# A four-layer graph network on one core: sorted blocks of 2500 edges, layer norms in one ScalarE pass

## The reference, cut to what matters

```python
h = jnp.maximum(_layernorm(x), 0.0)
x = x + gcn(h)             # normalized sum over the edges, @ W.T + b
h = jnp.maximum(_layernorm(x), 0.0)
x = x + attention(h)       # 4 heads of 32, softmax over the edges of a destination
h = jnp.maximum(_layernorm(x), 0.0)
x = x + weighted(h)        # two layers with edge weights, then a projection
h = jnp.maximum(_layernorm(x), 0.0)
xw = h @ W;  ew = edge_attr_16 @ edge_w        # [3125,128], [103125,128]
x = x + segment_sum(xw[src] * ew, dst) + b     # the edge layer
```

## Time and profile before

| | us |
|---|---|
| median of 3 runs | 2925.09 |
| lowest, highest | 2921.11, 2953.8 |
| the profiled execution | 2937.53 |
| its span | 2935.8 |
| PE busy in the span | 2349.3 (80%) |
| POOL busy | 1953.1 (67%) |
| DVE busy | 1910.0 (65%) |
| ScalarE (ACT) busy | 1408.7 (48%) |

### The profile page before, as it was taken

How to read it: one execution, slowest core, us unless ns; L and a number is a source line. 1 busy time by engine, 2 the same in 40 slices (tenths; PEclk the granted TensorE clock), 3 DMA queues, 4 the chain that set the end, 5 groups by cost and what they waited for, 6 DMA issues and landing times. The chain is left out here.

```text
span 2935.8 us, 64938 instructions
## 1 busy us (share of the span) xinstructions
PE 2349.3 (80%) x22192; PEld 1710.9 (58%) x22192; DVE 1910.0 (65%) x3810; ACT 1408.7 (48%) x2659; POOL 1953.1 (67%) x1608
## 2 busy tenths in 40 slices
PE   4677777766857777777788787889978999999998
PEld 2466666663424555555555555434546777777777
DVE  7999999983457777777777787211134555556555
ACT  0498988880038777777777775000003221222211
POOL 2278878805148888778777783577605888878874
PEclk7699999988968999988888899899987998999999
DMA  6267777768421111111111112996952222222213
GB/s 83 91 173 200 190 198 189 188 186 205 110 67 49 45 44 42 43 41 45 41 41 41 42 42 37 217 217 139 212 121 63 55 53 54 55 54 55 61 46 55
DMA packets 220459, 285.63 MB, mean 97 GB/s; under 512 B 130299, under 2 KB 166530, under 8 KB 217015
## 3 DMA queue, kind: packets, MB, share of 16 engines
q1 hardware_dynamic: 171548, 246.53, 33.8%
q0 software_dynamic: 48720, 36.84, 6.4%
HBM read 171.50 MB, written 112.09 MB: 97 GB/s over the span
## 5 line engine op out<-in xcount | busy, mean ns | idle before, releaser
L389 POOL DMA_INDIRECT scratch_slots<-sort_pay,sort_slot x400 | 590.0, 1475 | 185.2 <-issue 184.3
L1864 POOL TENSOR_TENSOR score<-score,rise 125x500 f32<-125x500 f32 (+1 forms) x609 | 671.9, 1139 | 52.5 <-DVE peaks L1800 48.5
L2399 POOL DMA_INDIRECT gathered_rows<-scratch_projected,src_i x425 | 532.4, 1253 | 156.7 <-issue 126.5
L1800 DVE CUSTOM_DVE_ANT_0 score<-raw,log_in 125x500 f32<-125x500 f32 (+1 forms) x609 | 353.9, 619 | 167.6 <-PE raw L1685 97.6
L1747 ACT ACTIVATE rise<-raw 125x1000 f32<-125x1000 f32 (+1 forms) x350 | 313.4, 918 | 183.1 <-DVE peaks L1800 95.7
L1700 PE MATMUL probsT<-ident,score 125*125 125x125 f32 x2175 | 363.8, 298 | 29.6 <-ACT score L1756 13.1
L1700 PEld LDWEIGHTS probsT<-ident,score 125*125 125x125 f32 x2175 | 304.3, 204 | 110.1 <-DVE weighed L1821 65.2
L874 PE MATMUL built<-pair_weight,hot 125*128 125x125 bf16 x3750 | 249.7, 229 | 63.9 <-DVE pair_weight L819 63.7
L1685 PE MATMUL raw<-QT,key 32*125 32x500 f32 (+1 forms) x1400 | 205.1, 657 | 94.8 <-DVE peaks L1800 90.8
L874 PEld LDWEIGHTS built<-pair_weight,hot 125*128 125x128 bf16 x3750 | 229.7, 103 | 75.8 <-DVE pair_weight L819 74.2
L1821 DVE COPY weighed<-probsT 125x500 f32<-125x500 f32 x400 | 251.1, 672 | 13.6 <-PE probsT L1700 13.6
(11 more groups left out here) (309 smaller groups left out, 4484.2 us busy)
## 6 DMA issues: line engine op xcount, KB each, us to landing
weights_in<-scratch_weightsT SPq DMA_DIRECT2D x50, 1093.8 KB
scratch_weightsT<-wT SPq DMA_DIRECT2D x25, 1367.2 KB
scratch_logs<-log SPq DMA_DIRECT2D x75, 437.5 KB
log_in<-scratch_logs SPq DMA_DIRECT2D x150, 218.8 KB
counts_in<-scratch_counts SPq DMA_DIRECT2D x25, 683.6 KB
scratch_counts<-cc SPq DMA_DIRECT2D x24, 683.6 KB
gathered_rows<-scratch_projected,src_i POOLq DMA_INDIRECT x425
scratch_slots<-sort_pay,sort_slot POOLq DMA_INDIRECT x400
```

The costliest lines, as they stand in the source:

```text
L389: nc.gpsimd.indirect_dma_start(rows, bass.IndirectOffsetOnAxis(ap=sort["slot"][:, b, c:c + 1], axis=0), pay[:, c, :], None).then_inc(sort[ ...
L1800: nc.vector.tensor_tensor_reduce(out=score[u][h][:, at:at + w], in0=raw[:, h, 0:w], in1=log_in[:, at:at + w], scale=1.0, scalar=-3e38, op0 ...
L1864: nc.gpsimd.tensor_tensor(score[u][h][:, at:at + w], score[u][h][:, at:at + w], rise[:, b, h, 0:w], ALU.add).then_inc(added, 1)
L2399: nc.gpsimd.indirect_dma_start(gathered[:, g % GATHERS, k, :], None, projected, bass.IndirectOffsetOnAxis(ap=src_i[:, FIRST + g, k:k + 1], ...
```

## The change

- **Blocks.** 24 blocks of 2500 edges, 60000 edges; 28 lists, of 128 slots each, without a second half. `REACH` is 88. A block is 7 rounds of four lists, 168 rounds in all; 69 groups are left for the gathers. Two blocks are placed together (`PER_BATCH`), so there are 12 batches of again 40 scatters: six in `adjacency`, one in `regular_gcn_layer`, five in `weighted_layers`.
- **Slots.** The four lists of a round lie in SBUF with the second pair at partition 64 once turned. The mixing is two matmuls, each of 36 partitions and 256 columns, into two banks. A block's slots are loaded in two DMAs with runs of 144 bytes, into four buffers instead of two; the first two loads stand in the prelude.
- **Edge stage.** The turned attributes share a bank with the turned slots, and their turn stands ahead of the block's sum. The first three gathers stand in the prelude. The rounding of the table runs in two interleaved strands.
- **Layer norm.** DVE's 25 subtractions are gone. `lift` = -mean / deviation is a bias, and ScalarE's pass becomes `Relu(scale * X + lift)`.
- **Bias.** `L3_gnn_b` starts the sums `acc` (on POOL) instead of being added to `X` (on DVE).
- **Semaphores** of the first layer are recorded and cleared later by POOL.

```diff
-SORT_BLOCKS = 10
-COLS = 40
+BATCHES = 12
+PER_BATCH = 2
+SORT_BLOCKS = BATCHES * PER_BATCH
+COLS = 20
-LISTS = 26
+LISTS = 28
-REACH = 168
+REACH = 88
-PLACED_IN_ADJACENCY = 5
+PLACED_IN_ADJACENCY = 6
...
-        for t in range(a, b):
-            nc.vector.tensor_scalar(H[:, t, :], X[:, t, :], mv[:, t, 0:1], 0.0, ALU.subtract, ALU.max)
         dve.wait_ge(std_ready, s + 1)
-        nc.vector.reciprocal(rstd[:, a:b], rstd[:, a:b]).then_inc(inv_ready, 1)
+        link(nc.vector.reciprocal(rstd[:, a:b], rstd[:, a:b]))
+        nc.vector.scalar_tensor_tensor(lift[:, a:b], mv[:, a:b, 0], -1.0, rstd[:, a:b], ALU.mult, ALU.mult).then_inc(inv_ready, 1)
...
-                    ins = nc.scalar.activation(H[:, t, :], H[:, t, :], ACT.Copy, scale=rstd[:, t:t + 1])
+                    ins = nc.scalar.activation(H[:, t, :], X[:, t, :], ACT.Relu, bias=lift[:, t:t + 1], scale=rstd[:, t:t + 1])
...
-    for c in range(COLS):
-        nc.gpsimd.indirect_dma_start(rows, bass.IndirectOffsetOnAxis(ap=sort["slot"][:, b, c:c + 1], axis=0), pay[:, c, :],
+    for c in range(PER_BATCH * COLS):
+        nc.gpsimd.indirect_dma_start(rows, bass.IndirectOffsetOnAxis(ap=slot[:, c:c + 1], axis=0), pay[:, c, :],
                                      None).then_inc(sort["placed"][u], 16)
...
-                    ins = nc.tensor.matmul(offset_ps[:], above16[:], in_list[:, :, :, c].rearrange("p b s -> p (b s)"),
-                                           start=(c == 0), stop=(c == COLS - 1))
+                    for u in range(2):
+                        ins = nc.tensor.matmul(offset_ps[:, u, 0:BATCHES * LISTS], above16[:],
+                                               in_list[:, BATCHES * u:BATCHES * (u + 1), :, c].rearrange("p b s -> p (b s)"),
+                                               start=(c == 0), stop=(c == COLS - 1))
...
-    PER_BLOCK = LISTS // 2
+    PER_BLOCK = LISTS // QUAD
+    BLOCK_BUFFERS = 4
+    HEAD_CHUNKS = 3
...
+        def load_block(sp, b):
+            u = b % BLOCK_BUFFERS
+            by_half = slots[b].rearrange("r (j l x) w -> r j l (x w)", l=2, x=2)
+            for half in range(2):
+                at = half * SECOND_ROWS
+                sp.dma_start(pay[:, u, :, at:at + 2 * SLOT], by_half[:, :, half, :]).then_inc(slots_in[u], 16)
...
+                pool.wait_ge(last["in"], 16 * LAST_LOADS)
+                pool.wait_ge(emptied, 1)
+                nc.gpsimd.tensor_scalar(acc[:], acc[:], last["bias"][:, 0:1], None, ALU.add)
+                pool.wait_ge(stored, 32)
+                for k in range(HEAD_CHUNKS):
+                    gather_chunk(0, k)
...
-                nc.vector.tensor_tensor(X[:], X[:], bias[:].unsqueeze(1).broadcast_to([P, TILES, D]), ALU.add)
...
                 def mix_attributes(r):
                     need(pe, s_copied, r)
-                    nc.tensor.matmul(mixed_ps[:], pay_t[:, r % 2, :], quad_mix[:].rearrange("r c d -> r (c d)"), start=True,
-                                     stop=True).then_inc(s_mixed, 1)
+                    for half in range(2):
+                        rows = slice(half * SECOND_ROWS, half * SECOND_ROWS + 2 * SLOT)
+                        ins = nc.tensor.matmul(mixed_ps[:, half, 0:2 * D], pay_t[rows, r % 2, :],
+                                               quad_mix[rows].rearrange("r c d -> r (c d)"), start=True, stop=True)
+                    ins.then_inc(s_mixed, 1)
...
+                    if r == -1:
+                        turn_attributes(0)
+                    if g is not None and g + 1 < ITEMS:
+                        turn_attributes(g + 1)
                     if here(r - 1):
                         sum_block(r - 1)
-                    if r == -1:
-                        turn_attributes(0)
                     if g is not None:
                         factors(g)
-                        if g + 1 < ITEMS:
-                            turn_attributes(g + 1)
```

More of the change, by code:

```diff
@@ L352, in _ @@
             sp.dma_start(table[ROWS:ROWS + GROWS, :], pad[:]).then_inc(table_done, 16)
-            with nc.allow_non_contiguous_dma(reason="runs of forty edges, and one destination of every block"):
+            with nc.allow_non_contiguous_dma(reason="runs of twenty edges, and one destination of every block"):
                 sp.dma_start(sort["base_i"][:], T["dst"][0:SORTED].rearrange("(o b r) -> o b r", o=1, r=BLOCK_EDGES)[:, :, 0]
@@ L2272, in _ @@
                     if r >= 2:
-                        pe.wait_ge(left, 2 * (r - 2) + 1)
+                        pe.wait_ge(left, 2 * r - 3 if r > 2 else 1)
                     for s in range(s0, s0 + n):
@@ L2652, in program @@
         rstd = keep(sb("rstd", [P, TILES]))
-        norm = (stats, mv, rstd)
+        lift = keep(sb("lift", [P, TILES]))
+        norm = (stats, mv, rstd, lift)
         ident = keep(sb("ident", [128, 128]))
```

285 lines of the change are left out of this document (165 added, 120 removed).

## The result

The changed kernel took 3114.3 us (median of 4 runs, 3091.76 to 3161.45) against 2930.23 us before: a ratio of 1.0589, with a 95% interval of 1.047 to 1.0709. The forecast was 2834 us, range 2785 to 2892. (Ratios with intervals leave out executions more than 1.5% above the fastest of their kernel; medians and ranges are over all.) The profiled execution took 3097.69 us, its span is 3095.9 us: 160.1 us longer than before's.

The account below looks back on a forecast made before the run. POOL's gathers bound the edge stage before, PE second; after the change PE (564 us) was to bind just ahead of POOL (560). Terms -110 - 11 + 11 + 10 + 12 - 5 + 2 = -91 us: 2834 us from 2925.09, range 2785 to 2892.

Parts of the forecast that it names:

- the one on the clock: Edge stage: lower clock mostly at the start and behind waits, so PE's 564 us become 578, -110 against 688.
- D: Edge-stage gathers slowed by a busier DVE at full price, 2.21 us each: 3036 us in all; chance 0.03.
- A round: Edge stage: PE's work for four lists was to take 2.44 us instead of 3.11, 168 times.
- The mixing: Edge-stage round: two matmuls on separate partitions and banks mostly overlap, 0.61 us instead of 0.92.
- B: Edge stage: the two mixing matmuls don't overlap, or mode changes eat it; round 2.75 us, 2886 us in all; chance 0.17.
- The block's sum: Edge-stage round: four matmuls of 88 columns, limited by loading weights, take 0.83 us instead of 1.19.
- A group: Edge stage: 625 gathered edges cost PE 1.04 for sums, 1.08 for factors, 0.11 for the turn: 2.23 us, 69 times.
- C: Edge-stage gathers slowed by a busier DVE: 2861 us at half price, chance 0.09; 2909 us in full, chance 0.07.
- The layer norms: Four norms: ScalarE takes over DVE's subtraction and maximum, second part 3.7 us earlier, on the path in three: -11 us.
- The prelude: PE's list offsets at 28.2 us instead of 21.83, and larger DVE passes over the lists: +11 us.
- The placement: POOL's scatters: a sixth batch in the adjacency, +10 us, and a fifth in the weighted layers, +12 us.
- The edge prelude: Before the edge stage: first slots loaded early, so PE's 7.05 us wait for that load shrinks: -5 us.

Follow-up runs that it names:

- session 3: Changed kernel unedited, 3143.92 us; changed kernel with 40-column sums, 3364.23 us; kernel before with 88-column sums, 3079.92 us; kernel before itself, 2920.59 us.
- session 1: Three edited versions of the changed kernel and one of the kernel before, 2877.08 to 2979.01 us by medians; kernel before 2897.26 us, changed kernel itself not run.
- the two lighter versions: Changed kernel with a group's sums behind the row matmuls, 2979.01 us; kernel before with block sums 88 columns wide instead of 168, 2939.95 us.
- the two denser ones: Changed kernel with mixing as one matmul of 100 rows and 512 columns, 2877.08 us; changed kernel with block sums 168 columns wide, 2904.99 us.
- sessions 2 and 4: Changed kernel rerun unedited, 2891.52 and 2862.04 us, beside edited versions; kernel before 2894.4 and 2894.44 us.
- the lightest: Changed kernel with block sums and their additions 40 columns wide instead of 88: 3364.23 us, ratio 1.1526.
- one mixing matmul: Changed kernel with mixing as one matmul over 100 rows and 512 columns instead of two: 2877.08 us, ratio 0.9928.
- the control: Changed kernel run again with no edit, beside edited versions: 2891.52 us, ratio 0.9859; its traced execution took 2854.61 us.
- session 5: Kernel before with an unused tile, 2897.52 us; kernel before with the new layer norm and later group sums, 2857.12 us; kernel before itself, 2893.45 us.
- the unused tile: Kernel before with one unused tile of 125 x 25 floats where the change has `lift`, no operation changed: 2897.52 us, ratio 1.0013.

## Why the prediction was wrong

**The step that failed** is the one on the clock: "The part at 1.2 GHz lies mostly at the start and behind waits, which a PE with its own limit has less of. I take 578 us". It gave the lower clock 14 us (578 for 564), less even than the 36 of the old mean of 0.94, and held a PE with its own limit to be a PE at full clock. Measured were 460 of 860 us at half clock and a mean of 0.74. The runs show that the load has a part in it. With the same instructions, fewer columns made both kernels slower in session 3: 80 fewer in the sum of the kernel before, the very sum that the change narrows, +5%; 48 fewer in that of the changed kernel +220 us by the medians. In session 1 the two lighter versions had 322 of 770 (in one of the longer runs) and 260 of 700 us at half clock, the two denser ones 13 of 647 and 18 of 670. None of the rivals had this mechanism; the one on the slower side (D) came nearest, 3036 against 3114, and that is luck, since the gathers took 1.23 us, less than before. In the traces of sessions 2 and 4 the step came true, with 14 to 16 us at half clock, nearly all at the start.

**What the load doesn't explain** is the session. Beside a kernel before of 2894 us the changed one took 2892 and 2862; beside one of 2921 or 2930 it took 3144 and 3114. Sessions 2 and 3 ran on a chip of the same number. The traces with long times at half clock are from the sessions that have late turns, though one of them, the kernel before with narrow sums in session 1, has only 6. What makes PE late there I didn't find. In those sessions the kernel before has its clock back within 2 to 16 us, the changed one and the narrow sums mostly within 14 to 122, the lightest never. The Trainium skill, page "TensorE: Matmul & The Clock Gate", section "Part 1: The HAM clock gate (the "warmup" mystery)", says that activity releases the throttle. The stage with sums of 40 columns doesn't agree, if activity is the busy time that the profile gives (its ends are modelled): 1132 busy us of 1136 released nothing. That the denser versions also hold the clock in a session like the third is likely from session 1, above all from one mixing matmul with its 37 late turns, but wasn't measured there. Nor was it separated what of the lighter work counts, the columns of the sum or the halved mixing: only the sum was varied beside a control.

**What the change would do at full clock**: there the trace of the control answers the forecast's steps.
- A round was to take 2.44 us and takes 2.66. The mixing is 0.63, forecast 0.61: the two matmuls do overlap (B is out). But spreading the sources ahead of it went from 0.22 to 0.32, which the sum left out; the two operations that the change put side by side have a price of 0.09 us a round, and a group's sum behind the mixing one of 0.10 (1.14 instead of the 1.04 that it takes behind one mixing matmul). The Trainium skill's rule that a change of the tiling mode drains the engine ("TensorEngine Tiling (Array Packing)", "Key Properties") would be a reason for it, which no run here shows, and is the small part of rival B that came true. The block's sum is 0.91, or 0.86 ahead of factors, forecast 0.83: weights do bound it, and a bit of streaming is left over.
- A group takes 1.14, 1.11 and 0.11, less the 0.05 of the sum ahead of it, 2.31; forecast 2.23. 168 x 2.66 + 69 x 2.31 = 606 us, and the stage took 618, forecast 578 with ends of 555 and 630.
- The gathers (C): 1.213 us with DVE busy 0.64 of the stage (394 of 618 us), 1.253 before at 0.56 in the first trace and 1.225 at 0.59 in session 5. A busier DVE didn't slow them. (The packets of the earlier trace rows, which rival D calls "up to 512 bytes", have 815 on average, 26.98 MB by 33110; nothing hangs on it.)
- The gain is smaller than it looks for one more reason: in the sessions with 2894 us the stage of the kernel before is itself 656 us, not 688 (read from the trace with the unused tile). There the change is worth -38.

**The layer norms**: forecast -3.7 each in three places and -11 in all, measured -1.6, -1.7 and -1.2. The step that was mis-sized is "ScalarE's pass is taken at its old price". 12 tiles took 4.72 us, 0.393 a tile, where the old pass had 0.30 (3.62 us for 12 in its timeline), and it now sets the second half's start: its square root waits at 2190.94 for the first half's pass. That the second half would start 3.7 us earlier was wrong too: 2191.66 - 2182.01 = 9.65 us from the norm's start, before 2200.60 - 2188.16 = 12.44, so 2.8. But with the same norm attention is 43 to 50 us shorter, which no step of the forecast had, and which is more than all that it was meant to bring.

**The prelude**: forecast +11, measured +13.1 up to its end. The offsets took 24.00 us, not 28.2: a column costs 1.8 ns. So the read of every twentieth element is cheaper than the nearest row said. The rest is not of the change alone: the first stage ended at 53.0 instead of 48.2 us in that trace, behind a load (`ends_i`) that came later, but at 48.0 in that of session 3 and at 54 in the kernel before with the norm alone. The change itself is nearer to +8: between the two traces of session 3 the prelude grew by 7.6.

**The first GCN layer** had no term, since its one batch stays one, and took 6.6 us more up to its sum; in the other traces of changed kernels it took 96 to 101 us, in those of the kernel before and its variants about 94. No run separates what of the change does it.

**The placement**: in the adjacency the last scatter was to start at about 679 us plus what the prelude costs, 13, and did at 692.6; the next stage came +10.6 later, forecast +10. In the weighted layers five batches took 341 us (forecast 342), but the first started 18.4 us after the norm instead of 11.5, because its attributes, now fetched in two pieces for each partition, took 15.2 us from issue to use against 9.9: +17, forecast +12. **The edge prelude** gave -2.3, forecast -5.

Put together, all terms but the edge stage and attention came to +40 us where +19 was forecast, attention gave 49 back, and the edge stage took 280 us more than its term.

## What to carry over

A busy TensorE is not a TensorE at full clock, and what its clock does can change with its load. Before making its matmuls smaller, look at how the time at half clock is spread over short stretches, and try the reverse on the chip: more columns of zeros, or a filling matmul. If that is faster, a saving there is a loss. And measure a change of this kind in more than one session: of this one a single session would have said -1% or +6%. The smallest version is as good as any: the kernel before with the new layer norm alone took 2849 us, ratio 0.9877 to the kernel before, where the changed kernel had 0.9892 beside it and 0.9859 in session 2, all within each other's intervals. It leaves the edge stage as dense as it was; in a session like that of the first measurement it wasn't measured.

## What was not expected of the hardware

PE at 0.50 for 1136 us on end while busy 1132 of them. A PE whose results come 1.8 us late at a recorded clock of 1.00. Late turns of slots in over a third of both kernels' rounds in two measurements, and in none of the ten traces of sessions 2, 4 and 5. Four matmuls of 88 columns with their own weights take 0.86 to 0.91 us, of 168 columns 1.19: half the columns save a quarter. A pass of ScalarE with a bias and a maximum costs 0.393 us for 125x128 values, one with a scale alone 0.30. And attention at a clock of 0.90 or 0.94, with the same work, depending on how the norm ahead of it was computed. I have no cause for that; the time of attention stayed the same over all the traces with the new norm (922 to 941 us) and the five without (960 to 981).
